# A decoder layer's last stage in f16 parts: three matmuls for one in gate, up and down, four tiles in flight, and GpSimd in the quantising

## The reference, cut to what matters

```python
def fp4_quant_dequant(x):                      # along the last dimension, BLOCK = 16
    xb = x.reshape(shape[:-1] + (shape[-1] // BLOCK, BLOCK))
    scale = jnp.maximum(jnp.max(jnp.abs(xb), axis=-1, keepdims=True) / 6.0, 1e-12)
    idx = jnp.searchsorted(_MID, jnp.abs(xb / scale))
    return (_GRID[idx] * jnp.sign(xb / scale) * scale).reshape(shape)
def fp4_linear(x, w):
    return jnp.einsum('bsk,nk->bsn', fp4_quant_dequant(x), fp4_quant_dequant(w))
gate, y = fp4_linear(x, w_gate), fp4_linear(x, w_up)        # 512 -> 1408
out = fp4_linear(jax.nn.silu(gate) * y, w_down)             # 1408 -> 512
x = x + attention(_layernorm(x)); x = x + cross_attention(ctx, _layernorm(x)); x = x + ffn(_layernorm(x))
```

## Time and profile before

| | |
|---|---|
| median of 3 runs | 5284.13 us (5282.34 to 5284.47) |
| profiled execution | 5280.23 us, span 5278.4 us |
| PE busy | 5016.3 us (95%) |
| DVE busy | 4163.2 us (79%) |
| ACT busy | 2899.9 us (55%) |
| POOL busy | 2707.6 us (51%) |
| granted TensorE clock, mean | 0.983 |

### The profile page before, as it was taken

How to read it: one execution, slowest core, us unless ns; L and a number is a source line. 1 busy time by engine, 2 the same in 40 slices (tenths; PEclk the granted TensorE clock), 3 DMA queues, 4 the chain that set the end, 5 groups by cost and what they waited for, 6 DMA issues and landing times. The chain is left out here.

```text
span 5278.4 us, 97228 instructions
## 1 busy us (share of the span) xinstructions
PE 5016.3 (95%) x27884; PEld 2067.5 (39%) x27884; DVE 4163.2 (79%) x7250; ACT 2899.9 (55%) x5206; POOL 2707.6 (51%) x988
## 2 busy tenths in 40 slices
PE   5998899999999999999999999999968999999999
PEld 2444233333333333333333333333315555555555
DVE  6556688888888888888888888888836777777776
ACT  2222167777767777677777777777653333333332
POOL 3000187888878788888878888787860000000000
PEclk8999799999999999999999999999988999999999
DMA  3443377767767776776777676777660000000000
GB/s 113 133 124 109 87 171 173 170 169 175 171 168 171 174 173 167 177 168 171 168 176 172 167 178 166 174 167 174 153 157 23 18 18 24 18 18 18 24 18 12
DMA packets 210097, 660.66 MB, mean 125 GB/s; under 512 B 25668, under 2 KB 105156, under 8 KB 152198
## 3 DMA queue, kind: packets, MB, share of 16 engines
q0 software_dynamic: 64512, 469.79, 38.3%
q1 hardware_dynamic: 145159, 185.65, 11.6%
HBM read 123.56 MB, written 61.64 MB: 35 GB/s over the span
## 5 line engine op out<-in xcount | busy, mean ns | idle before, releaser
L831 DVE TENSOR_REDUCE rowmax_parts<-scores_qk 128x1 f32<-128x512 f32 x4096 | 2523.1, 678 | 465.1 <-PE scores_qk L904 465.1
L811 ACT ACTIVATE probs_T<-scores_kq 128x512 f32<-128x512 f32 x4096 | 2286.3, 596 | 979.7 <-PE scores_kq L904 914.9
L745 POOL TENSOR_TENSOR probs_added<-probs_added,probs_T 128x2048 f32<-128x2048 f32 x448 | 2030.3, 4532 | 457.2 <-ACT probs_T L811 445.8
L904 PE MATMUL scores_kq<-q_operand,k_operand 103*128 103x512 f16 (+3 forms) x3712 | 1274.6, 349 | 11.0 <-ACT probs_T L811 9.1
L904 PE MATMUL scores_qk<-k_operand,q_operand 96*128 96x512 f16 (+4 forms) x3712 | 1123.1, 352 | 43.3 <-DMA k_operand<-positions_dram 19.7
L975 PE MATMUL outputs_T<-probs_T,v_operand 128*32 128x512 f32 x8192 | 1091.9, 605 | 1.3 <-ACT probs_T L811 1.3
L904 PEld LDWEIGHTS scores_kq<-q_operand,k_operand 103*128 103x128 f16 x3712 | 358.6, 97 | 921.8 <-ACT probs_T L811 636.6
L1423 PE MATMUL f_gate_up<-w_gate_up,xq_T 128*128 128x352 f32 x2048 | 627.2, 462 | 0.8 <-issue 0.8
L904 PEld LDWEIGHTS scores_qk<-k_operand,q_operand 96*128 96x128 f16 (+1 forms) x3712 | 354.8, 98 | 438.3 <-DVE rowmax_parts L831 184.3
L1423 PEld LDWEIGHTS f_gate_up<-w_gate_up,xq_T 128*128 128x128 f32 x2048 | 382.5, 190 | 202.1 <-issue 2.8
L745 POOL TENSOR_TENSOR probs_added<-probs_T 128x2048 f32<-128x2048 f32 x64 | 290.3, 4536 | 239.1 <-ACT probs_T L811 239.1
(11 more groups left out here) (155 smaller groups left out, 3938.2 us busy)
## 6 DMA issues: line engine op xcount, KB each, us to landing
probs_poured<-probs_T POOLq DMA_DIRECT2D x448, 1024.0 KB, 7.2
qk_parts_dram<-qk_parts SPq DMA_DIRECT2D x96, 256.0 KB, 2.6
q_operand<-qk_parts_dram SPq DMA_DIRECT2D x192, 128.0 KB, 2.6
k_operand<-qk_parts_dram SPq DMA_DIRECT2D x192, 128.0 KB, 3.2
v_dram<-v_heads SPq DMA_DIRECT2D x16, 1024.0 KB, 5.7
v_operand<-v_dram SPq DMA_DIRECT2D x64, 256.0 KB, 5.9
q_operand_above<-qk_parts_dram SPq DMA_DIRECT2D x96, 128.0 KB, 2.8
x_groups<-x SPq DMA_DIRECT2D x8, 1024.0 KB, 9.3
```

The lines of the kernel that those rows point to most:

```text
L745: nc.gpsimd.tensor_tensor(total, first, probs[:, b % PBUF, :], ALU.add).then_inc(added.sem, 1)
L811: nc.scalar.activation(probs[:, kb % PBUF, qt * BANK:(qt + 1) * BANK], pb[:, k % 2, :], ACT.Exp)\
L831: nc.vector.reduce_max(rowmax[:, w % 2, c // NQ, c % NQ:c % NQ + 1], pa[:, k % 3, :], AX.X)\
L904: return nc.tensor.matmul(out, lhsT, rhs, start=start, stop=stop, skip_group_check=True)
```

## The change

In `finish`, the products of gate, up and down are made of f16 parts, three matmuls for one, as the projections are. The quantised weights are scaled by 64 and split in `project`: ScalarE writes the high part, VectorE the low part, in the room of the f32 ones (`f16_parts`). The quantised x and h are split per tile: ScalarE copies the high part ("high x", "high h0", "high h1"), GpSimd subtracts for the low part ("low x", "low h0", "low h1"); both parts are turned by f16 transposes. Gate and up go in five pieces of 256 columns and one of 128, h is quantised in two halves of 768 and 640. The add into x2 and four of x's quantising passes go to GpSimd, the norms' last pass to ScalarE. Down has a PSUM bank of its own. The `warm` instructions aren't in any order any more. Each engine has its own order over four tiles, written out for all 32 (no hardware loop).

In `project`, GpSimd's two weight passes become one VectorE pass, and each weight job gets a low-part pass by VectorE; `JOB_AT` and `JOB_TURN` move. In `prepare`, the positions are spread over 128 partitions.

```diff
+def f16_parts(x):
+    dims = " ".join("abcde"[:len(x.shape) - 1])
+    return x.bitcast(F16).rearrange(f"{dims} (s f) -> {dims} s f", s=2)
...
-        pos16 = sb("pos_parts", [1, 8, L], F16)
+        pos16 = sb("pos_parts", [P, 8, L // P], F16)
-            sp.dma_start(pos_scr.rearrange("(o r) n -> o r n", o=1), pos16[:, :, :]).then_inc(stored, 16)
+            sp.dma_start(pos_scr.rearrange("r (p i) -> p r i", p=P), pos16[:, :, :]).then_inc(stored, 16)
...
-JOB_AT = (0, 1, 3, 5, 7, 8)
-JOB_TURN = 3
+JOB_AT = (0, 2, 4, 5, 6, 7)
+JOB_TURN = 4
...
-                nc.gpsimd.tensor_scalar(w[:, :, own], w[:, :, own], UPSCALE, None, ALU.mult).then_inc(w_scaled, 1)
-                nc.gpsimd.tensor_tensor(w_parts[:, 1, :, own], w[:, :, own], w_parts[:, 0, :, own], ALU.subtract)\
+                nc.vector.scalar_tensor_tensor(w_parts[:, 1, :, own], w[:, :, own], UPSCALE, w_parts[:, 0, :, own],
+                                               ALU.mult, ALU.subtract).then_inc(w_lo, 1)
...
+                            wait_apart(dve, w_copied, w_copied.at(n, number + 1), passed)
+                            nc.vector.scalar_tensor_tensor(
+                                turned_to(kind, row, width, 1), wt[:, 0:width].rearrange("p (c q) -> p c q", q=P), UPSCALE,
+                                turned_to(kind, row, width, 0), ALU.mult, ALU.subtract).then_inc(w_copied_lo.sem, 1)
...
-                                pe.wait_ge(w_copied.sem, w_copied.at(n, number))
+                                pe.wait_ge(w_copied_lo.sem, w_copied_lo.at(n, number))
...
+FW = 2 * P
+PIECES = [(k * FW, min(FW, FF - k * FW)) for k in range(-(-FF // FW))]
+HALVES = ((0, 3 * FW), (3 * FW, FF - 3 * FW))
+ORDER_PE = (
+    ("turn h 0", -2), ("project", 1), ("ff2", -1), ("ff3", -1), ("turn h 1", -2), ("ff4", -1), ("turn q", 1),
+    ("turn h 2", -2), ("ff5", -1), ("down1", -2), ("logits", 1), ("down2", -2), ("turn x", 0), ("down0", -2),
+    ("ff1", 0), ("turn probs", 1), ("ff0", 0), ("cross", 1),
+)
+ORDER_DVE = (
+    ("gate1", -1), ("gate0", -1), ("measure cross", 0), ("measure out", 1), ("shift cross", 0), ("scale x", 0),
+    ("gate2", -1), ("shift out", 1), ("gate3", -1), ("exponents x", 0), ("quantise h0", -1), ("gate5", -1),
+    ("gate4", -1), ("softmax", 1), ("quantise h1", -1), ("sum probs", 1), ("scale cross", 1), ("add down", -2),
+)
+ORDER_ACT = (
+    ("silu0", -1), ("high h1", -2), ("copy hT 0", -2), ("root cross", 0), ("root out", 1), ("norm cross", 0),
+    ("silu2", -1), ("silu3", -1), ("copy hT 1", -2), ("norm out", 1), ("copy hT 2", -2), ("copy q", 1),
+    ("silu4", -1), ("silu5", -1), ("high x", 0), ("copy xT", 0), ("exp", 1), ("copy probs", 1), ("high h0", -1),
+    ("silu1", 0),
+)
+ORDER_POOL = (
+    ("add cross", 0), ("low h1", -2), ("divide x", 0), ("round x", 0), ("low x", 0), ("low h0", -1),
+)
...
+def over_tiles(order, slot):
+    for i in range(-3, NT + 3):
+        for kind, ahead in order:
+            if 0 <= i + ahead < NT:
+                slot(kind, i + ahead)
...
+                elif kind == "divide x":
+                    x_inverted.passed(pool, n)
+                    nc.gpsimd.tensor_scalar(x_inv[:, :], x_inv[:, :], SHADE, None, ALU.mult).then_inc(x_shaded.sem, 1)
+                    normed[1].passed(pool, n)
+                    x_shaded.passed(pool, n)
+                    x_lo.passed(pool, n - 1)
+                    nc.gpsimd.tensor_tensor(by16(xq[:, :]), by16(ln[1][:, :]), wide(x_inv[:, :]), ALU.mult)\
+                        .then_inc(x_divided.sem, 1)
+                elif kind == "round x":
+                    x_rounder.passed(pool, n)
+                    nc.gpsimd.tensor_tensor(xq[:, :], xq[:, :], x_m[:, :], ALU.add).then_inc(x_added.sem, 1)
+                    x_added.passed(pool, n)
+                    nc.gpsimd.tensor_tensor(xq[:, :], xq[:, :], x_m[:, :], ALU.subtract).then_inc(x_rounded.sem, 1)
+                    x_rounded.passed(pool, n)
+                    nc.gpsimd.tensor_tensor(by16(xq[:, :]), by16(xq[:, :]), wide(x_scale[:, :]), ALU.mult).then_inc(x_quant.sem, 1)
+                elif kind in ("low h0", "low h1"):
+                    h_hi[i].passed(pool, n)
+                    nc.gpsimd.tensor_tensor(h16[:, 1, a:a + w], hq[:, a:a + w], h16[:, 0, a:a + w], ALU.subtract)\
+                        .then_inc(h_lo[i].sem, 1)
...
+                if kind == "project":
+                    got[n % 2].passed(pe, n // 2)
+                    x_scaled.passed(pe, n - 1)
...
+                elif kind == "turn x":
+                    x_lo.passed(pe, n)
+                    xq_copied.passed(pe, n - 1)
...
+                            last = nc.tensor.transpose(px[:, c, part, :], x16[:, part, c * P:(c + 1) * P], ident16[:, :])
...
+                        for a, b in PRODUCTS:
+                            last = nc.tensor.matmul(pd[:, :], hT[:, c, a, :], wd[:, c, b, :],
+                                                    start=opens and c == first and a == b,
+                                                    stop=ends and c == first + count - 1 and a == 1)
...
+                            for a, b in PRODUCTS:
+                                last = nc.tensor.matmul(pg[:, k % 2, g, 0:w], xqT[:, n % 2, c, a, :],
+                                                        w_up[:, c, g, b, at:at + w],
+                                                        start=c == 0 and a == b, stop=c == KT - 1 and a == 1)
```

More of the change, by code:

```diff
@@ L282, in jobs, with turned_to @@
             return tiles
+        def turned_to(kind, row, width, part):
+            if kind == 2:
+                return down_T[:, part, 0:width // P, :]
+            return f16_parts(wgu[:, :, :, :])[:, 0:KT, kind, part, bass.ds(row * P, P)]
         def over_groups(eng, group):
@@ L1133, in finish @@
[L1133 to L1154 removed]
+        pg = ps("f_gate_up", [P, 2, 2, FW], F32)
@@ L1257, in _ @@
+            over_tiles(ORDER_ACT, slot)
         @block.vector
```

547 lines of the change are left out of this document (315 added, 232 removed).

## The result

| | before | after |
|---|---|---|
| median of 4 runs each, side by side | 5283.24 us (5279.42 to 5284.47) | 5072.82 us (5064.90 to 5075.51) |
| ratio, 95% interval | | 0.960 (0.958 to 0.962) |
| profiled execution | 5280.23 us, span 5278.4 us | 5071.46 us, span 5069.4 us |
| start of the span to attention's first product | 579.6 us | 600.6 us |
| attention, up to TensorE's first matmul of the last stage | 3374.7 us | 3370.6 us |

The kernel is 4% faster, 10 us from the forecast of 5063. The lower rows of the table say more than the sum does: the last stage gained 225.9 us where 199 were forecast, and the first stage lost 21.0 where 20 were to be gained. Two errors, of 27 and 41 us, stand against each other.

The account below looks back on a forecast made before the run. TensorE was taken to bound the last stage, VectorE second. 5278.4 - 199 (last stage) - 20 (first stage) = 5059 us of span; with 1.8 around it and 3.9 for the median, given as 5063; range 4995 to 5190.

Parts of the forecast that it names:

- TensorE per tile: Last stage: TensorE's work falls from 38.5 us a tile; two sums gave 30.7 and 32.0, 31.5 taken.
- VectorE per tile: Last stage: VectorE's passes fall from 30.6 to 23.7 us a tile; with 45 links of 0.03, 25.1.
- The port stalls: Last stage: GpSimd's 10.3 us of passes a tile cost VectorE 5.3 us, bounds 0 and 10.3.
- The period: Last stage: 40.24 us a tile becomes 33.8 (31.8 to 38); TensorE's walk gave 32.4, VectorE's 32.9.
- A: Last stage: the port costs nearly nothing, TensorE alone sets 32.3 us a tile; 46 us less, 5017; chance 0.20.
- B: Last stage: every GpSimd pass stops VectorE in full, period 38 us; 130 us more, 5193; chance 0.15.
- C: Last stage: waiting TensorE drops to 1.2 GHz; 7 of 31 periods cancel the gain, 10 give 5378; chance 0.04.
- The table loads: Last stage, ScalarE: a load starts only after the wait ahead of its function, adding 1.28 us, four a tile.
- The signs: Last stage: wrong if 256-column matmuls exceed 0.13 us, GpSimd's 512-wide passes 1.6, VectorE's table-load idle 4 a tile.
- Fill and drain: Last stage: tile 0's step over at 4005, 10 us less for first and last steps, drain 36, end 5079.
- The first group: First stage: first product at 38; moving weight splitting to VectorE gains 16 to 20 us, 20 taken.
- Later groups: First stage: the 1.35 us stall goes, about as much returns at the third job; 0 a group (-2 to +2).

Follow-up runs that it names:

- the bank of its own: Changed kernel with the output projection writing PSUM bank 1 of f_logits instead of bank 0: 5024.81 us.
- the better order: Changed kernel with weight jobs behind products 0, 1, 4 (were 0, 2, 4), measuring and norm at 7 and 9 (were 4, 6): 5028.85 us.
- the split before the turn: Changed kernel, quantised weights split in SBUF by ScalarE and GpSimd before turning: 5109.8 us; plus projection's own bank 5068.25; plus later measuring and norm 5013.53.
- four kernels with the same last stage: Changed kernel with, singly: no low-part weight pass 5009.51 us; jobs at other products 5028.85; GpSimd's two weight passes 5084.86; weights split before turning 5109.8.

## Why the prediction was right or wrong, step by step

**Right in the sum, by two errors that cancel.** 5063 was forecast, 5072.8 came. Its terms were -199 and -20; they measured -225.9 and +21.0, with -4.1 in attention. That the total came within 10 us is luck. (The terms as written, 5059 + 1.8 + 3.9, make 5065.)

**TensorE per tile: right, 0.5 us too high.** 31.5 us were taken and 31.5 measured, but some 0.45 of these are half clock, which the sum hadn't; at full clock TensorE is busy 31.92 - 0.92 = 31.0, and with the bank of its own 30.8, next to the lower of the two sums. Transposes came at 0.056 for 0.06. The Trainium skill, "TensorE: Matmul & The Clock Gate", section "Back-to-back issue gap", gives 81 ns for a sustained stream of 128-column load and matmul pairs; the trace, now with many of them in a row (0.056 us each), doesn't bear that out. (The 592 ns that the text gives down are the row of the output projection; down's has 599, and 299.0 us busy for 632, so 10.4 us a tile and not 9.6.)

**VectorE per tile: right.** 23.7 us bare were forecast; 27.5 less 3.9 of stalls are 23.6.

**The port stalls: right in kind, 1.4 us too high.** 5.3 were taken and 3.9 measured; the roundings and low x cost 2.5 for 3.6 (3.6 + 1.2 - 1.4 is 3.4, by the text's own figures), low h0 1.4 for 1.7. The text takes GpSimd's passes whole. What VectorE loses is the part that GpSimd still has to go when VectorE's pass starts: 0.45, 0.79, 0.88, 0.98 and 1.57 us for the five passes that meet one, as means of the steady stretch, each less 0.14 to 0.19. Between the bounds of 0 and 10.3 the count of who meets whom by the orders came near: GpSimd's add into x2, low h1 and divide x, which lie beside VectorE's passes out of PSUM and its measuring, cost nothing.

**The period: mis-sized by 1.4 us, 43 us in all.** 33.8 were taken, 32.4 measured. The walk along the two loops gave 32.4 and 32.9, and I put 0.9 on top for their beating against each other in a fixed order. That VectorE's loop is the longer one is right, and it closes on the very step that the walk names, "scale cross" ahead of the projection, with one wait of 0.92 us a tile for 0.4. Its terms in a tile at full clock (VectorE's timeline from 4387.9 to 4419.8): bare passes 23.6 for 23.7, links 1.0 for 1.4, the port 3.9 for 5.3, waits 3.4 for 2.5 (0.88 for the projection, 0.96 for the norm, 0.81 for GpSimd's add, 0.72 for silu), 31.9 for 32.9. The allowance of 0.9 measured nothing. Half clock adds 0.45 on average. So the terms that were too high are the allowance, 0.9, and the port, 1.4, with 0.4 in the links; the waits and the clock, too low by 0.9 and 0.45, hide half of it.

**The rivals.** The period came out at A's 32.3, but not by A's mechanism: the port costs 3.9 us, and VectorE's loop, not TensorE alone, sets it. B's full 10.3 us didn't come. C's mechanism took part with 0.45 us a tile; it was priced as a period wholly at half clock, and came as 3 us of one.

**The table loads: the rule fails.** By the row at 28.64 a load was to start only once the wait ahead of its function is over. In the last stage it starts ahead of that wait:

```profile
4419.98 1.28 ACT L1332 ACT_TABLE_LOAD   x1
...
4422.69 0.30 ACT L1332 ACTIVATE std_f<-mean_var_f,eps_f 128x1 f32<-128x1 f32 x1 [1.44 <-DVE mean_var_f L1421]
```

The load is over at 4421.26, and the root still waits 1.44 us for VectorE. There are four loads a tile, as forecast; VectorE's idle time for ScalarE is 1.7 us a tile, far from the 4 that would have shown the forecast wrong.

**The signs.** One that was to show the forecast wrong did come: a 512-wide pass of GpSimd over 1.6 us, its scaling one with 1.65. It cost nothing here, as 0.59 of it is its own waiting for VectorE.

**Fill and drain: 17 us too low.** 1098.2 - 31 x 32.40 = 93.8 us lie around the 31 periods; the forecast's 1124.7 less 31 x 33.8 leave 76.9. The last tiles were not short by 10 us: near the end TensorE waits for VectorE's gates (2.18 us at 5004.01, 1.89 at 5030.65) and for the parts of h (5.14 at 5053.50).

**The first group: right.** First product at 38.84 for 38, second group's turn 20.0 us earlier for 20; with the weight passes back on GpSimd 23.7 of it are gone again.

**Later groups: the step that failed.** "0 a group (-2 to +2)" measured 4.3 a group for five groups and 9.8 for the two with six jobs, 41 us in all. The text names the right mechanism, the third job's turn waits for the second's low pass behind a 7.5 us quantising, and then gives it the size of the stall at 143.16 without walking it as it walked the first group. Walked, the pass starts after quantising and norm, and costs what it is late: 3.9, with 1.4 at the second job. And the last two groups, with twice the jobs, weren't looked at: there 20 us stay even in the better order.

**prepare: right.** TensorE's first matmul is at 32.62 us, for 32.49 before.

**Attention** was to stay. It is 4.1 us shorter. It measured 3376.1 to 3376.6 in the three kernels with the split before the turn and 3370.2 to 3371.4 in all others with the change; what moves it was not tried.

## What to carry to other kernels

Where work is added to an engine's order, walk every kind of group once, the steady one and the fullest, and see what stands ahead of the added step and who waits for it: at the same amount of work the order was worth 35 us here. When two engines' loops are only a microsecond apart in length, look for the buffer that ties them; another half-tile of PSUM was worth 40 to 47 us, more than taking 4.8 us of work a tile off TensorE, which lost 19. Check a total stage by stage before it is taken for a confirmation.

## What the runs showed of the hardware

The granted clock can fall for a short stretch within a stage whose mean is 0.99. Behind a single wait of 0.92 us the projection ran at 1.2 GHz in 8 of 30 tiles (in 4 or 5 in four kernels with the same last stage); behind 1.22 us, with the rest of TensorE's work the same, in 28 of 30; behind 2.37 us, with less work and three more waits in the tile, in 22 of 30; without the wait in none of 29. One such stretch costs 1.7 us, and it makes the time of a stage vary by several us between kernels that don't differ in it (1090.5 to 1098.2).

GpSimd's passes over 512 columns of f32 took 1.06 (L1294) to 1.65 us (groups by shape, 4100 to 5000; the longest):

```profile
L1302 POOL TENSOR_TENSOR x_quantised<-x_quantised,x_scale 128x512 f32<-128x512 f32 x28 | 46.3, 1652 | 2.2
```

VectorE's passes that met GpSimd's got longer by 0.3 to 1.4 us: by what the GpSimd pass had left when they started, less about 0.15 us. GpSimd's passes stand still behind VectorE's in the same way (1.65 us for 1.06). The Trainium skill, "SBUF — State Buffer", section "Who interferes with whom", has the shared port as a lock for the whole instruction. The trace of the last stage agrees with that to 0.15 us. The first stage of the kernel before shows one exception, and with it the row at 65.14 that the prediction couldn't place: beside GpSimd's scaling pass over 2048 columns (51.23 to 56.60) VectorE's two-input pass of 51.72, 0.69 us bare, is through at 55.41 after 3.69, so it ran again some 1.9 us before that pass ended, while its next pass, with one input, took 1.43 us for a bare 0.43 and so was held until 0.15 us before the end. From 60.75 to 66.28 it is the same: the two-input pass of 61.10 is free 1.9 us before the end, and the next one, at 65.14, is not held at all. Over the whole tile VectorE lost 3.9 us for 11.1 of GpSimd's work, as much of that lies beside passes of VectorE that don't meet it.

A pass of ScalarE that scales and shifts 512 columns (the norm, 28 tiles, two a tile) takes 814 ns, where a copy of as many takes 586.
